# FFN gates as tanh on ScalarE with the add and multiply on VectorE, in two halves

## The reference

```python
gate = fp4_linear(x, w_gate)          # 128 -> 352
y = fp4_linear(x, w_up)               # 128 -> 352
h = jax.nn.silu(gate) * y
return fp4_linear(h, w_down)          # 352 -> 128
```

## Time and profile before

| | us |
|---|---|
| median of 3 runs | 1923.89 (1923.73 to 1925.67) |
| the profiled execution | 1927.78 |
| its span, first to last instruction | 1926.1 |
| busy PE, ACT, DVE, POOL | 1650.8, 1454.4, 1183.6, 269.2 |
| mean granted TensorE clock | 0.952 |

### The profile page before, as it was taken

The page is one execution under the profiler, slowest core; times in us unless marked ns, Lnnn a source line. Parts: engine busy times, 40 slices in busy tenths (PEclk is TensorE's granted clock), DMA queues, the critical chain, the costliest instruction groups (busy, mean ns, idle before and its releaser), DMA issues. The chain is left out here.

```text
span 1926.1 us, 33412 instructions
## 1 busy us (share of the span) xinstructions
PE 1650.8 (86%) x12948; PEld 634.7 (33%) x12948; DVE 1183.6 (61%) x2132; ACT 1454.4 (76%) x2513; POOL 269.2 (14%) x292
## 2 busy tenths in 40 slices
PE   5599999999999999754889888898789888883995
PEld 3122222222222222241334332433233332222673
DVE  7999999999999998467264535445345433223220
ACT  4188777787787778623999999999999999992221
POOL 4400000000000000022000100010001013312466
PEclk9699999999999999976999999999999999996998
DMA  5201111111111110003111221113111223231423
GB/s 171 91 26 49 38 43 38 38 43 37 38 38 43 38 41 19 24 7 129 37 49 58 88 70 50 50 55 110 39 34 61 93 77 105 97 118 44 136 55 31
DMA packets 69839, 115.85 MB, mean 60 GB/s; under 512 B 9689, under 2 KB 54597, under 8 KB 65072
## 3 DMA queue, kind: packets, MB, share of 16 engines
q1 hardware_dynamic: 58416, 92.87, 15.2%
q0 software_dynamic: 11264, 20.83, 4.0%
HBM read 71.49 MB, written 42.14 MB: 59 GB/s over the span
## 5 line engine op out<-in xcount | busy, mean ns | idle before, releaser
L750 ACT ACTIVATE rows_and_probs<-psS 128x512 f32<-128x512 f32 x1024 | 556.4, 596 | 178.6 <-PE psS L648 176.9
L772 DVE TENSOR_REDUCE max_of_halves<-psM 128x2 f32<-128x1024 f32 x512 | 617.6, 1222 | 44.8 <-PE psM L617 15.5
L1556 ACT ACTIVATE exps<-cpsS 128x1024 bf16<-128x1024 f32 x512 | 540.1, 1086 | 26.9 <-PE cpsS L1323 24.9
L1323 PE MATMUL cpsS<-rotary_stack 128*128 128x512 bf16 x1024 | 304.0, 386 | 69.9 <-ACT exps L1556 28.3
L668 PE MATMUL psO<-rows_and_probs,plain_v 128*9 128x256 f32 x4096 | 317.0, 381 | 4.9 <-issue 2.2
L1566 ACT ACTIVATE cprobs<-cpsS 128x1024 f32<-128x1024 f32 x256 | 277.1, 1082 | 19.7 <-PE cpsO L1356 17.2
L1303 PE MATMUL cpsS<-rotary_stack 128*128 128x512 bf16 (+3 forms) x768 | 195.9, 332 | 63.8 <-ACT exps L1556 37.7
L617 PE MATMUL psM<-plain_top 64*128 64x512 bf16 x1024 | 208.9, 389 | 25.1 <-DVE max_of_halves L772 24.8
L648 PE MATMUL psS<-plain_top 64*128 64x512 bf16 x1024 | 213.0, 387 | 6.7 <-issue 6.5
L648 PE MATMUL psS<-plain_rest 64*128 64x512 bf16 x1024 | 207.2, 377 | 0.0
L1356 PE MATMUL cpsO<-cprobs,rotary_v 128*9 128x512 f32 (+3 forms) x1536 | 154.5, 490 | 0.6 <-DVE rotary_sums L1880 0.6
(11 more groups left out here) (295 smaller groups left out, 1692.5 us busy)
## 6 DMA issues: line engine op xcount, KB each, us to landing
rotary_stack<-q_parts SPq DMA_DIRECT2D x48, 192.0 KB
rotary_stack<-k_parts SPq DMA_DIRECT2D x48, 192.0 KB
rotary_stack<-q_rot_parts SPq DMA_DIRECT2D x48, 192.0 KB
rotary_stack<-k_rot_parts SPq DMA_DIRECT2D x48, 192.0 KB
tokens_taken<-parts_and_sums POOLq DMA_DIRECT2D x32, 259.0 KB, 4.2
plain_top<-q_parts SPq DMA_DIRECT2D x64, 96.0 KB
plain_top<-k_parts SPq DMA_DIRECT2D x64, 96.0 KB
e_x<-tokens_taken SPq DMA_DIRECT2D x8, 518.0 KB, 11.5
```

The costliest lines, as they stand in the source:

```text
L750: act.activation(pr[n % SLOTS_P][:, h, :], psS[u % RING][:, :], ACT.Exp, scale=SCALE).then_inc(s_e, 1)
L772: dve.tensor_reduce(mh[g % 2][:, :, hh, t, kh:kh + 1].rearrange("p e o -> p (e o)"), psM[n % 2][:, :, :], AX.X, ALU.max).then_inc(s_r, 1)
L1323: ins = pe.matmul(to[:, kh, :], q[:, x, y_ * P:(y_ + 1) * P], k[:, x, kh * CH:(kh + 1) * CH], start=True, stop=True)
L1556: act.activation(ex[d % EX][:, :, :], psS[n % 3][:, :, :], ACT.Exp, scale=SCALE, accum_out=den[:, at:at + 1]).then_inc(s_e, 1)
```

## The change

The silu is computed as gate * (1 + tanh(gate / 2)) / 2. ScalarE computes tanh(gate / 2); VectorE adds 1 and multiplies by the gate in one operation; the factor 0.5 goes into the multiplication with "up", which becomes an operation with one more operand.

In batches 1 to 3 the task "silu" is replaced by two halves, each a "bend" (ScalarE, tanh over 4 x 352 = 1408 columns into the buffer `bent`, which lies in the area of the transposed hidden units) and a "blend" (VectorE). Both halves use the same buffer, so the second bend waits for the first blend. An "up" tile waits for the blend of its half only. The planner gets 2.0 for a bend and 1.6 for a blend, where the silu had 6.0.

In batch 0 ScalarE writes the tanh of each gate tile from PSUM to a buffer in the room of the attention's probabilities (`first_bent`), and VectorE computes (1 + tanh) * gate from that and PSUM into `gate`. The gate's bank is so kept by VectorE and no longer by ScalarE.

```diff
@@ -1019,9 +1019,12 @@
         tasks.append((("x", n, c), "slot", 0.7, [("round_x", n, c)], 0.0))
     for t in range(TB):
         tasks.append((("g", n, t), "slot", 0.5, [("x", n, t // TC)], 0.0))
-    tasks.append((("silu", n), "other", 6.0, [("g", n, t) for t in range(TB)], 0.0))
+    if n:
+        for c in range(2):
+            tasks.append((("bend", n, c), "other", 2.0, [("g", n, t) for t in range(TB)] + [("blend", n, i) for i in range(c)], 0.0))
+            tasks.append((("blend", n, c), "vector", 1.6, [("bend", n, c)], 0.0))
     for t in range(TB):
-        tasks.append((("u", n, t), "slot", 0.5, [("silu", n)] if n else [("g", n, t)], 0.0))
+        tasks.append((("u", n, t), "slot", 0.5, [("blend", n, t // TC)] if n else [("g", n, t)], 0.0))
         if t % 2:
             if n == 0 and t // 2 < SHARED:
                 tasks.append((("scale_h", n, t // 2), "vector", 4.0, [("u", n, t), ("u", n, t - 1)], 0.0))
@@ -1172,7 +1175,7 @@
 
     by_act, kept_at, counts = set(), {}, {"dve": 0, "act": 0}
     for label, k in use.items():
-        act_keeps = label[1] == 0 and label[0] in ("x", "g", "h", "px")
+        act_keeps = label[1] == 0 and label[0] in ("x", "h", "px")
         if act_keeps:
             by_act.add(label)
         engine = "act" if act_keeps else "dve"
@@ -1244,6 +1247,7 @@
         raw = y[:, 0:4, :]
         s_f, s_kd, s_ka = sem("banks_filled"), sem("banks_kept_by_dve"), sem("banks_kept_by_act")
         s_d, s_rows, s_si, s_hq = sem("dve_steps"), sem("rows_ready"), sem("gates_made"), sem("hidden_quantised")
+        s_bl, s_bt = sem("gates_blended"), sem("first_gates_bent")
         s_hs, s_hp = sem("hidden_scaled"), sem("first_hidden_steps")
         s_y, s_p1, s_p2 = sem("quotients_ready"), sem("part1_made"), sem("part2_made")
         s_p0, s_rest = sem("part0_made"), sem("rests_made")
@@ -1257,6 +1261,17 @@
         block = c.enter_context(nc.Block())
         KEPT = 12
         BLOCKS = 2 * I // QB
+
+        bent = ht_area[:, 0:TC * I].rearrange("p (t i) -> p t i", i=I)
+
+        def first_bent(t):
+
+            at = 2 * I + 2 * BLOCKS + t % 2 * I
+            return pr[t // 4][:, t // 2 % 2 * 2:t // 2 % 2 * 2 + 2, :, :].rearrange("p h b n -> p (h b n)")[:, at:at + I]
+
+        def blends(n, t):
+
+            return (n - 1) * 2 + t // TC + 1
 
         def first_hidden(i):
 
@@ -1508,9 +1523,14 @@
 
             def work(label):
                 kind, n = label[:2]
-                if kind == "silu" and n:
+                if kind == "bend":
                     wait_kept(act, ("g", n, TB - 1))
-                    act.activation(gate[:, :, :], gate[:, :, :], ACT.Silu).then_inc(s_si, 1)
+                    if label[2]:
+                        act.wait_ge(s_bl, blends(n, 0))
+                    act.activation(bent, gate[:, label[2] * TC:(label[2] + 1) * TC, :], ACT.Tanh, scale=0.5).then_inc(s_si, 1)
+                elif kind == "g" and n == 0:
+                    act.wait_ge(s_f, use[label] + 1)
+                    act.activation(first_bent(label[2]), bank(label)[:, 0:I], ACT.Tanh, scale=0.5).then_inc(s_bt, 1)
                 elif kind in ("a", "s") and n == 0:
                     u = unit_at[label]
                     if u == 0:
@@ -1534,8 +1554,6 @@
                         if kind == "px":
                             wait_read(act, ("u", n, cc * TC + TC - 1))
                         act.activation(xt[:, cc * CH:(cc + 1) * CH], bank(label), ACT.Copy).then_inc(s_ka, 1)
-                    elif kind == "g":
-                        act.activation(gate[:, label[2], :], bank(label)[:, 0:I], ACT.Silu).then_inc(s_ka, 1)
                     else:
                         t = label[2]
                         if t >= TC:
@@ -1810,6 +1828,10 @@
                     stats_of(n, label[2])
                 elif kind == "stats_out":
                     stats_out(n, label[2])
+                elif kind == "blend":
+                    dve.wait_ge(s_si, (n - 1) * 2 + label[2] + 1)
+                    at = slice(label[2] * TC, (label[2] + 1) * TC)
+                    dve.scalar_tensor_tensor(gate[:, at, :], bent, 1.0, gate[:, at, :], ALU.add, ALU.mult).then_inc(s_bl, 1)
                 elif kind == "bias":
                     add_bias(n)
                 elif kind == "base":
@@ -1836,13 +1858,19 @@
                         if cc == 0:
                             for i in range(STORES):
                                 dve.wait_ge(s_st[i], 16 * len(range(i, 8 * n, STORES)))
-                        dve.tensor_copy(gate[:, cc, :], bank(label)[:, 0:I]).then_inc(s_kd, 1)
+                        if n:
+                            dve.tensor_copy(gate[:, cc, :], bank(label)[:, 0:I]).then_inc(s_kd, 1)
+                        else:
+                            dve.wait_ge(s_bt, cc + 1)
+                            dve.scalar_tensor_tensor(gate[:, cc, :], first_bent(cc), 1.0, bank(label)[:, 0:I],
+                                                     ALU.add, ALU.mult).then_inc(s_kd, 1)
                     elif kind == "u":
                         if n:
-                            dve.wait_ge(s_si, n)
+                            dve.wait_ge(s_bl, blends(n, cc))
                         else:
                             wait_kept(dve, ("g", n, cc))
-                        dve.tensor_tensor(gate[:, cc, :], gate[:, cc, :], bank(label)[:, 0:I], ALU.mult).then_inc(s_kd, 1)
+                        dve.scalar_tensor_tensor(gate[:, cc, :], bank(label)[:, 0:I], 0.5, gate[:, cc, :],
+                                                 ALU.mult, ALU.mult).then_inc(s_kd, 1)
                     elif kind == "h":
                         if cc >= TC:
                             wait_read(dve, ("d", n, 0))
```

## The result

The changed kernel takes 1914.32 us in the median of five runs (1912.49 to 1916.04), the kernel before 1923.73 us in five (1922.09 to 1925.67). The ratio is 0.9945, with a 95% interval of 0.9934 to 0.9956: 9.4 us faster, where 1915.4 us was forecast. The profiled execution took 1912.5 us with a span of 1910.8; it is the fastest of the five, and the profiled execution of before was slower than all timed ones of that kernel, so the two traces stand 15.3 us apart and not 9.4. Which part of that belongs to the change has to be read stage by stage.

The account below looks back on a forecast made before the run. ScalarE's queue was taken to bound the second attention stage. Stops -8.2, clock -1.0, hand-over +0.3 and batch 0 +0.4 gave -8.5 us, from 1923.9 to 1915.4 us, range 1911.5 to 1920.5.

Parts of the forecast that it names:

- The bound: Second attention stage: ScalarE's queue sets its length, busy 801.3 of 846 us, so whatever leaves it shortens the kernel.
- The price of the stop: Batches 1 to 3: silu with two table loads, 5.27 us, becomes two tanh, 2.54 us; 8.2 us saved in all.
- The clock term: Behind the three stops: TensorE hardly stands still and keeps its clock; gain 1.0 us, bounds 0 to 3.9.
- The sign of full clock behind the sites: Check in the trace: TensorE's windows behind the three silu sites would be at full clock.
- the two idle sums together under 46.6 us: Check in the trace: ScalarE's idle before L1556 and L1566 together would fall below 46.6 us.
- The 1.31 us wait: ScalarE's wait for TensorE shortly after a stop; three times it gave the clock gain's upper bound, 3.9 us.
- The hand-over: Between the tanh halves: exps cover VectorE's blend; small stalls cost 0.3 us over three sites, bounds 0 and 2.
- the first rival: Three sites: half the gain lost on hand-overs, three waits of 1.6 us, no clock gain; 1920.9 us; chance 0.11.
- Batch 0: First gates: VectorE's additions run beside ScalarE's tanh, only the one behind the last tanh counts; 0.4 us cost.
- The second rival: Batch 0: VectorE's additions stand in line with the products, +4.2 in place of +0.4; 1919.2 us; chance 0.06.
- The first exp: Check at the start of the second attention: it would come at 906.7 us; 910 would mean additions in line.
- The sum: Whole kernel: -8.2 - 1.0 + 0.3 + 0.4 = -8.5 us, so a median of 1915.4 us.

Follow-up runs that it names:

- e1: Changed kernel with batch 0's gates back to silu on ScalarE, tanh halves only in batches 1 to 3; 10.5 us under the kernel before, ratio 0.9943.
- e7: Changed kernel with silu in place of tanh in each half, so table loads return; 7.9 us over the kernel before, ratio 1.0042.
- e9: Kernel before with two whole tanh of 2816 columns, one behind the other, for each wide silu; 1.4 us under the kernel before, ratio 0.9992.
- e2: Batch 0 as in the changed kernel, the body with the wide silus of the kernel before; 1.0 us over the kernel before, ratio 1.0000.
- e4: Changed kernel with planner costs of 0.01 for bend and blend, so no exp stands between the halves; 2.1 us over the kernel before, ratio 1.0011.
- e5: The changed kernel run once more, unaltered; 12.2 us under the kernel before, ratio 0.9937.
- e3: Kernel before with one tanh of 2816 columns for each wide silu, add and multiply left out; 7.4 us under the kernel before, ratio 0.9958.
- e10: Changed kernel with no exp between the halves, but each half in its own bf16 buffer; 3.2 us under the kernel before, ratio 0.9984.

## Why the prediction was right

1. *The bound.* ScalarE's queue sets the body's length: shown from three sides. 2.8 us less per stop (e1), 2.9 more per half (e7), the same length from other work (e9), each passed on within about 2 us of the sum over all sites.
2. *The price of the stop.* Forecast 5.27 - 2.54 = 2.7 us for each batch, 8.2 in all. Measured 5.34 - 2.54 = 2.80 and 8.4; up to the 641st exp all that is not waiting became 8.7 to 9.3 us shorter, so 0.3 to 0.9 us have no row. The tanh held the queue for 1.27 us as forecast. No load came with it: ahead of the runs only the Trainium skill ("ScalarE: Activation LUTs", section "Table sets: the hidden batching unit") had tanh in the set of exp, and the rows of loads agree. The body of the three executions with the changed code is 10.0 us shorter in the mean (827.8 against 837.8 twice).
3. *The clock term, -1.0 us.* The size fits, the reason is not borne out, and so the fit is in part luck. The sign of full clock behind the sites came: 1.00 from 910 to 1580 us in all three traces of the changed code, where it had fallen behind each of the three stops before. Up to the 641st exp the waits fell from 30.8 and 30.9 us (before, e2) to 29.1 to 29.3, by 1.6 us: the 2.8 us right behind the stops went, and 1.2 us came elsewhere with the new plan. But a shorter stop alone brings no net gain: with the whole tanh, behind which TensorE stood 1.70 to 2.75 us in place of 4.55 to 5.59, the clock fell behind two stops of three and the waits are 31.3 and 31.4 us. And with the halves a long stop costs nothing: in e7 TensorE stood up to 4.00 us, the clock fell three times, and the waits are 29.2 us as in the changed kernel. What the waits follow is the plan, and not TensorE's stand or its clock. The 1.31 us wait behind one stop of one trace, which was read as a cost of stops, is 0.33 us in e2, whose body has the same code. The sign that the prediction named for this term, the two idle sums together under 46.6 us, failed as it was put: they are 47.1 us. They hold the idle ahead of the first exp, which grew from 10.9 to 12.5 us when the load in it went; the prediction had counted all 46.6 us into the stage, and the sign should have been read from the first exp on.
4. *The hand-over, +0.3 us.* No wait before any second tanh. The cover was named rightly and e4 gave the price without it, but that was too low in the first rival: 4.8 us for ScalarE's waits alone, where 13.2 came, since waits for TensorE added more than the wait itself.
5. *Batch 0, +0.4 us.* 0.6 in the mean of the traces, nothing in the time (e2). The second rival's 4.2 us in line did not come: VectorE's additions ran beside ScalarE's tanh. The first exp was put at 906.7 and came at 904.2, since all before it ran 1.3 us earlier in that execution and TensorE got through the first five gates in 4.73 us in place of 5.38.
6. *The sum.* Forecast were 8.5 us, measured 9.4; the other comparisons of the same body gave 12.2 (e5) and 10.5 (e1), so the single time could have come 3 us lower. Measured term by term: stops 8.4 (forecast 8.2), waits 1.6 (1.0, for another reason), hand-over nothing (0.3 against), batch 0 0.6 against (0.4), and the 0.3 to 0.9 us without a row. Up to the 641st exp the three executions with the changed code are 10.4 to 10.8 us under the two with the wide silus.

## What to carry to other kernels

When one engine's queue sets a stage, price an instruction by the stop that it makes between its neighbours, from start to start, loads and lost overlap included; a function from the loaded set with two cheap operations on an idle engine can be shorter than the function itself. When such a step is cut in two with a hand-over between, what has to be checked is not the cost of the halves but the work that stands between them, and who else stands behind the second engine's queue: with the same instructions and no room the kernel lost all that it had won. Before a term of a microsecond or two is believed or given up, run the same kernel twice and compare stretch by stretch: here the body scattered by 2.7 us and more with the same code, but most of that lay in one stretch behind the sites, and up to there a difference of 2 us stood out clearly.

## What the runs showed of the hardware

- An ACTIVATE's recorded duration creeps up while the engine is never idle: in the changed kernel the exps go from 1.07 us at 943.76 to 1.15 us at 954.88, while they start every 0.90 or 1.00 us; after a gap it is 1.02 us again. This is why the six tanh have a mean of 1433 ns in the rows and hold the queue for 1.27 us. Start to start is the price.
- A scalar_tensor_tensor in f32 costs what the tensor_tensor costs: 1.63 us for 1408 columns where 1.61 was worked out, 0.52 us for 352 columns with one operand in PSUM. With the tanh in bf16 two of them took 3.16 us, 1.58 each: nothing to gain.
- TensorE's clock behind a stand: it fell to 0.50 for 3 us or more after 1.70 and 2.75 us (e3), 3.38, 3.92 and 4.00 us (e7), 4.29, 4.44 and 5.33 us (e9) and 4.55, 4.71 and 5.59 us (before) of idle, and stayed at 1.00 after 1.86 us (e3), 2.59 us (e10) and 2.83 us (e7). The length of one stand alone does not tell. The first matmul behind it can hide the fall: it took 0.39 us for 512 columns after 3.38 us (e7) and 4.44 us (e9), as at full clock, while the granted clock of the 2.5 us from its start was 0.56 and 0.60.
